# An embedding gather on GpSimd: its scratch writes and its holds give way to answers from SyncE

## The chip, the cores and the metric

One Trainium2 chip, of which the kernel uses 1 core. The metric is device time in microseconds (us), lower is better. The 16 DMA engines of the core serve all its queues. The work is done by TensorE (PE in the rows; PEld are its weight loads), VectorE (DVE), ScalarE (ACT) and GpSimd (POOL); SyncE (SP) only issues transfers.

## The reference

A recommendation model (DLRM style) for 512 samples, all in float32:

```python
B, NF, D, V, NDENSE = (512, 26, 64, 12500, 13)
h = relu(dense @ dw1 + db1)
dense_emb = relu(h @ dw2 + db2)                       # [512, 64]
sparse_emb = emb_tables[f_ids, sparse_idx]            # 26 rows of 64 floats for each sample
emb = concatenate([dense_emb[:, None, :], sparse_emb], axis=1)    # [512, 27, 64]
inter = einsum('bfd,bgd->bfg', emb, emb)
pairs = inter[:, iu0, iu1]                            # the 351 pairs above the diagonal
z = concatenate([emb.reshape(512, -1), pairs], axis=1)
z = relu(z @ ow1 + ob1)                               # 2079 -> 512
z = relu(z @ ow2 + ob2)                               # -> 256
z = relu(z @ ow3 + ob3)                               # -> 128
y = z @ ow4 + ob4                                     # -> 1
```

An index may be negative or too large; the kernel wraps and clamps it as the reference's indexing does.

## The kernel before

The 512 samples are four tiles (`t` = 0 to 3) of 128, one sample per partition. Every engine has one hand-written program, and semaphores alone set the order between them.

**GpSimd** issues 104 gathers (L211), 26 per tile, one per field. Each is an indirect DMA that brings one row of 64 floats for each of the 128 samples. The fields of a tile form four groups: `s` = 0 to 7, 8 to 15, 16 to 23, and 24 and 25. Each group has a semaphore of its own, which counts landed gathers. Behind nearly every gather stands a memset of 128x192 bytes of `pace` (L219), a scratch tensor that nothing reads; the last eight gathers of the last tile have none. In tiles 1 to 3, two gathers, `s` = 7 and `s` = 10, carry a second semaphore, `gathers_held`, and instead of a memset they are followed by a wait (L217): GpSimd stands still until TensorE has finished the first or the second half of the previous tile's interactions (`inter_done`).

**TensorE** does the following for tile `t`, in this order. `turn(t, g)` waits for group `g` and transposes its rows into a PSUM bank (L240). ScalarE (groups 0 and 2, L386 and L387) or VectorE (groups 1 and 3, L465 and L466) copies the bank into `emb`, twice. `field_products(t, g)` waits for these copies (`kept`) and multiplies them with the weights into `acc[t]` (L259), two fields at a time. `interactions(t, 0)` and `interactions(t, 1)` are 128 small products each as the trace counts them (L276), one half of the tile's samples each. ScalarE and VectorE then copy each half into `pairs` (`moves`, L392 and L182), and `pair_product(t)` (L292) adds them to `acc[t]`. The tiles overlap by a fixed list:

```python
for t in range(TILES):
    if t:
        interactions(t - 1, 0)
    turn(t, 0)
    if t:
        interactions(t - 1, 1)
    field_products(t, 0)
    if t:
        pair_product(t - 1)
        z1_to_features(t - 1, at_once)
    turn(t, 1)
    ...field_products(t, 1), turn(t, 2), field_products(t, 2), turn(t, 3), field_products(t, 3)
```

Both halves wait on `gathers_held` (L272): `interactions(t, 0)` may start only when GpSimd has issued gather `s` = 7 of the next tile and holds behind it, `interactions(t, 1)` only when it has issued `s` = 10. So no gather instruction runs beside an interaction block. The last tile's interactions come when all gathers are over and have no such wait. Layers 2 to 4 run for tiles 0 to 2 together inside the last tile, and for tile 3 at the end.

**ScalarE** works in this order around a tile's start: `moves(t - 1, 0)`, `keep(t, 0)` (the copies of group 0), `moves(t - 1, 1)`. **VectorE** first makes the row numbers of the gathers. **SyncE** issues the indices' and the first layer's weights' transfers (L190 to L194), then waits for the result (L195).

Of the kernel before, what the change touches and what calls it, by code (L numbers as in the profile page):

```python
# [7 lines left out]
NF = 26  # L8
# [6 lines left out]
P = 128  # L15
TILES = B // P
LAST = TILES - 1
# [20 lines left out]


EARLY = LAST * P  # L40
PACE = 192
HOLDS = [7, 10]
UNPACED_FROM = 18
Z1_STEPS = [(0, 1), (1, 2), (2, 4)]
K1 = H1 // P

# [21 lines left out]
def build(nc, idx, tables, dense_pack, small_pack, w1, out):  # L68
    with ExitStack() as ctx:
        def sb(name, shape, dt=F32):  # L70
            return ctx.enter_context(nc.sbuf_tensor(name, shape, dt))
# [4 lines left out]
        def sem(name):  # L76
            return ctx.enter_context(nc.semaphore(name))
# [5 lines left out]
        table_base = sb("table_base", [P, TILES, NF], I32)  # L83
        rows = sb("rows", [P, TILES, NF], I32)
        gathered = sb("gathered", [P, TILES, NF, D])
        pace = sb("pace", [P, TILES * NF, PACE], mybir.dt.uint8)
        dense_sb = sb("dense_sb", [D, DENSE_COLS])
        small = sb("small", [P, SMALL_COLS])
        dense_h = sb("dense_h", [D, B])
# [33 lines left out]
        dense_act = sem("dense_act")  # L123
        ones_set = sem("ones_set")
        group_in = [[sem(f"group_in{t}_{g}") for g in range(NG)] for t in range(TILES)]
        gathers_held = sem("gathers_held")
        group_turned = sem("group_turned")
        kept_act = sem("kept_act")
        kept_dve = sem("kept_dve")
# [1 line left out]
        inter_done = sem("inter_done")  # L131
# [56 lines left out]
        @block.sync  # L188
        def _(sp):
            sp.dma_start(idx_raw[:, 0:1, :], idx[:, 0:1, :]).then_inc(idx_in, 16)  # L190
            sp.dma_start(idx_raw[:, 1:TILES, :], idx[:, 1:TILES, :]).then_inc(later_idx_in, 16)
            for g in range(W_GROUPS):
                groups = slice(g * W_GROUP, (g + 1) * W_GROUP)
                sp.dma_start(w[:, groups, :], w1[:, groups, :]).then_inc(w_in[g], 16)  # L194
            sp.wait_ge(y_done, 2)  # L195
            sp.dma_start(out, y[:]).then_inc(y_out, 16)
            sp.wait_ge(y_out, 16)

        @block.gpsimd
        def _(pool):  # L200

            nc.gpsimd.iota(table_base[:], pattern=[[0, TILES], [V, NF]], base=0,
                           channel_multiplier=0).then_inc(base_made, 1)
            pool.wait_ge(rows_ready, 1)
            for t in range(TILES):
                if t == 1:
                    pool.wait_ge(rows_done, 1)
                for g, (c0, c1) in enumerate(GROUPS):
                    for s in range(2 * c0, 2 * c1):
                        held = t > 0 and s in HOLDS  # L210
                        pool.indirect_dma_start(  # L211
                            out=gathered[:, t, s, :], out_offset=None, in_=tables,
                            in_offset=bass.IndirectOffsetOnAxis(ap=rows[:, t, s:s + 1], axis=0),
                            engine_sem=gathers_held if held else None,
                        ).then_inc(group_in[t][g], 16)
                        if held:
                            pool.wait_ge(inter_done, 2 * (t - 1) + HOLDS.index(s) + 1)  # L217
                        elif t < LAST or s < UNPACED_FROM:
                            nc.gpsimd.memset(pace[:, t * NF + s, :], 0)  # L219

        @block.tensor
        def _(pe):
# [25 lines left out]
            def kept(t, g):  # L248

                pe.wait_ge(kept_dve if g % 2 else kept_act, t * 2 + g // 2 + 1)  # L250
                if t == LAST and g == NG - 1:
                    pe.wait_ge(kept_act, t * 2 + 3)
# [9 lines left out]
            def interactions(t, k):  # L262

                if k == 0:
                    if t == 0:
                        pe.wait_ge(dense_placed, 1)
                    kept(t, 2)
                    kept(t, 3)
                    if t:
                        moved(t - 1)  # L270
                if t < LAST:
                    pe.wait_ge(gathers_held, 2 * t + k + 1)  # L272
                for n in range(HALF):
                    for j in range(4):
                        b = t * P + j * GROUP + k * HALF + n
                        mm = nc.tensor.matmul(inter[k][QUAD * j:QUAD * j + PLACES, n * PLACES:(n + 1) * PLACES],  # L276
                                              emb[0:D, b, :], emb[0:D, b, :], start=True, stop=True)
                mm.then_inc(inter_done, 1)

            def moved(t):  # L280

                pe.wait_ge(moved_act, t + 1)
                pe.wait_ge(moved_dve, t + 1)
# [48 lines left out]
# [11 lines that stand above are left out]
                if t < LAST:  # L343
                    field_products(t, 1)
                    turn(t, 2)
                    field_products(t, 2)
                    turn(t, 3)
                    field_products(t, 3)
# [9 lines left out]
            turn(LAST, 3)  # L358
            c0, c1 = GROUPS[2]
            interactions(LAST, 0)  # L360
            field_products(LAST, 2, (c0, c0 + 2))
            interactions(LAST, 1)
# [209 lines left out]
```

## Time and profile before

| | |
|---|---|
| median of 3 runs | 188.66 us (187.79 to 189.02) |
| the profiled execution, its own time | 187.21 us |
| its span, first to last instruction | 185.4 us |
| PE busy | 127.4 us (69%) |
| POOL busy | 123.8 us (67%) |
| mean granted TensorE clock | 0.88 of full speed |
| gathers | 104, 951 ns mean, 98.9 us in all |
| scratch memsets | 90, 274 ns mean, 24.7 us in all |

A busy time says how long an engine worked, not whether anyone waited for it. The profile's chain of waits follows the work that ended last back through what released each step, and gives each its start and length. A timeline gives an engine's instructions in order of time; the brackets name how long the engine was idle before one and what released it. "Issue" is time for which the profile shows no releaser.

### The profile page before, as it was taken

What the parts mean: (1) busy time and instruction counts of PE and PEld (TensorE: products, weight loads), DVE (VectorE), ACT (ScalarE), POOL (GpSimd) and SP (SyncE); (2) the same over time, 40 slices, a digit from 0 to 9 for tenths busy, and PEclk for the clock granted to TensorE, in tenths of its full rate; (3) what the DMA queues carried; (4) which work ended last, traced back from release to release, by engine and by line L of the source; (5) the groups of instructions that cost most, each with busy time, mean ns of one, the idle gap of its engine ahead of it and who ended that gap; (6) DMA issues with size and microseconds to landing.
All of it is one profiled execution on the core that took longest, in us unless ns stands there. A gap on an engine that the chain in (4) does not pass through costs nothing.

```text
span 185.4 us, 3069 instructions
## 1 busy us (share of the span) xinstructions
PE 127.4 (69%) x1301; PEld 68.8 (37%) x1301; DVE 37.8 (20%) x97; ACT 42.2 (23%) x96; POOL 123.8 (67%) x199
## 2 busy tenths in 40 slices
PE   1510285828655995839439993959729979989994
PEld 0000132514344442524226432424426446656453
DVE  2700003000142204100144005000234023136011
ACT  0440310031046201040075001040174011166011
POOL 3888888888735888888565888888367887200000
PEclk9999999975965699996965798587997999999999
DMA  5999532221212332312312332222222324100000
GB/s 157 409 332 357 172 26 23 23 28 21 21 13 23 21 22 24 28 22 26 24 13 24 23 27 20 23 28 20 19 20 20 22 25 31 18 4 0 4 0 0
DMA packets 4576, 9.80 MB, mean 53 GB/s; under 512 B 2065, under 2 KB 2065, under 8 KB 3922
## 3 DMA queue, kind: packets, MB, share of 16 engines
q0 software_dynamic: 3328, 3.41, 21.3%
q1 hardware_dynamic: 1010, 5.30, 7.1%
q10 hardware_dynamic: 224, 0.89, 1.6%
q8 instruction: 10, 0.16, 0.4%
q14 instruction: 4, 0.03, 0.1%
HBM read 9.59 MB, written 0.00 MB: 52 GB/s over the span
## 4 chain that ended last, share of the span: by engine, by line
PE 45%; POOL 26%; issue 18%; ACT 5%; DMA 3%; DVE 2%
PE acc L259 20%; POOL gathered L211 20%; PE acc L292 10%; PE inter L276 7%; POOL pace L219 6%; PE acc L310 4%; DMA gathered<-tables,rows 2%; ACT emb L386 1%; ACT emb L387 1%; PE turned L240 1%; PE acc L301 1%; ACT pairs L392 1%; DMA idx_raw<-idx 1%; ACT z L399 1%; DVE emb L466 1%
## 5 line engine op out<-in xcount | busy, mean ns | idle before, releaser
L211 POOL DMA_INDIRECT gathered<-tables,rows x104 | 98.9, 951 | 34.6 <-issue 16.9
L259 PE MATMUL acc<-w,emb 128*128 128x512 f32 x104 | 65.7, 780 | 19.4 <-issue 12.3
L259 PEld LDWEIGHTS acc<-w,emb 128*128 128x128 f32 x104 | 31.3, 315 | 46.3 <-issue 36.9
L392 ACT ACTIVATE pairs<-inter 28x96 f32<-28x96 f32 (+1 forms) x64 | 15.7, 246 | 39.8 <-PE inter L276 39.1
L219 POOL MEMSET pace<- 128x192 uint8 x90 | 24.7, 274 | 0.1
L292 PE MATMUL acc<-w,pairs 128*128 128x512 f32 x56 | 24.7, 592 | 0.0
L182 DVE COPY pairs<-inter 28x96 f32<-28x96 f32 (+1 forms) x64 | 17.0, 266 | 26.5 <-PE inter L276 25.8
L276 PE MATMUL inter<-emb 64*28 64x28 f32 x1024 | 12.6, 204 | 13.8 <-DMA gathered<-tables,rows 10.1
L240 PE MATMUL turned<-small,gathered 128*128 128x128 f32 x52 | 10.1, 317 | 13.5 <-DMA gathered<-tables,rows 13.5
L386 ACT ACTIVATE emb<-turned 128x512 f32<-128x512 f32 x8 | 8.8, 1098 | 45.7 <-issue 28.6
L465 DVE COPY emb<-turned 128x512 f32<-128x512 f32 (+1 forms) x7 | 5.5, 784 | 64.1 <-issue 49.5
L276 PEld LDWEIGHTS inter<-emb 64*28 64x28 f32 x1024 | 11.3, 116 | 18.1 <-DMA gathered<-tables,rows 10.6
L292 PEld LDWEIGHTS acc<-w,pairs 128*128 128x128 f32 x56 | 10.6, 190 | 12.9 <-issue 12.2
L240 PEld LDWEIGHTS turned<-small,gathered 128*128 128x128 f32 x52 | 6.9, 158 | 18.6 <-issue 13.2
L399 ACT ACTIVATE z<-acc 128x512 f32<-128x512 f32 (+2 forms) x6 | 2.5, 456 | 34.8 <-PE acc L292 25.4
L387 ACT ACTIVATE emb<-turned 64x512 f32<-64x512 f32 x8 | 8.8, 1096 | 0.1
L478 DVE COPY z1t<-acc 128x512 f32<-128x512 f32 x3 | 2.1, 692 | 31.5 <-issue 20.4
L310 PE MATMUL acc<-z1t,small 128*128 128x384 f32 (+1 forms) x32 | 7.5, 387 | 0.3 <-issue 0.3
L310 PEld LDWEIGHTS acc<-z1t,small 128*128 128x128 f32 x32 | 4.8, 191 | 2.5 <-issue 0.6
L466 DVE COPY emb<-turned 64x512 f32<-64x512 f32 (+1 forms) x7 | 5.5, 790 | 0.1
L224 PE MATMUL inter<-dense_sb 13*64 13x512 f32 x2 | 2.0, 1084 | 4.0 <-DMA dense_sb<-dense_pack 4.0
L227 PE MATMUL inter<-dense_h,dense_sb 64*64 64x512 f32 x2 | 2.0, 1084 | 2.1 <-ACT dense_h L376 2.1
(47 smaller groups left out, 26.3 us busy)
## 6 DMA issues: line engine op xcount, KB each, us to landing
w<-w SPq DMA_DIRECT2D x5, 1024.0 KB, 8.7
gathered<-tables,rows POOLq DMA_INDIRECT x104, 3.4
small<-small_pack ACTq DMA_DIRECT2D x1, 706.5 KB, 6.0
dense_sb<-dense_pack ACTq DMA_DIRECT2D x1, 160.5 KB
idx_raw<-idx SPq DMA_DIRECT2D x1, 39.0 KB
idx_raw<-idx SPq DMA_DIRECT2D x1, 13.0 KB, 1.9
out<-y SPq DMA_DIRECT2D x1, 2.0 KB
```

Source lines behind the costliest of these rows:

```text
L182: last = copy(pairs[QUAD * q:QUAD * q + PLACES, t, 0:top, first:first + HALF], src)
L211: pool.indirect_dma_start(out=gathered[:, t, s, :], out_offset=None, in_=tables, in_offset=bass.IndirectOffsetOnAxis(ap=rows[:, t, s:s + 1 ...
L219: nc.gpsimd.memset(pace[:, t * NF + s, :], 0)
L240: mm = nc.tensor.transpose(turned[g % 2][:, (c - c0) * P:(c - c0 + 1) * P], gathered[:, t, 2 * c:2 * c + 2, :].rearrange("p f d -> p (f d) ...
L259: nc.tensor.matmul(acc[t][:], emb[:, tile_of(t), place(2 * c)], w[:, c, :], start=(c == 0), stop=False)
L276: mm = nc.tensor.matmul(inter[k][QUAD * j:QUAD * j + PLACES, n * PLACES:(n + 1) * PLACES], emb[0:D, b, :], emb[0:D, b, :], start=True, sto ...
L292: mm = nc.tensor.matmul(acc[t][:], pairs[:, t, s, :], w[:, FIELD_CHUNKS + s, :], start=False, stop=(s == SLOTS - 1))
L310: mm = nc.tensor.matmul(banks[m][:, 0:n], ow2[:, k, m * P:(m + 1) * P], z1t[:, k, samples], start=(k == 0), stop=(k == K1 - 1))
L386: nc.scalar.activation(evens(t, g), turned_all(g), ACT.Copy)
L387: nc.scalar.activation(odds(t, g), turned_odds(g), ACT.Copy).then_inc(kept_act, 1)
L392: last = move(lambda dst, src: nc.scalar.activation(dst, src, ACT.Copy), t, k, (0, 1))
L466: nc.vector.tensor_copy(odds(t, g), turned_odds(g)).then_inc(kept_dve, 1)
```

## The change

The memsets, the scratch tensor and both kinds of hold go: GpSimd no longer waits for `inter_done`, TensorE no longer for `gathers_held`. Instead every gather adds 1 to `gathers_issued`, SyncE waits for each such step and adds 1 to `echo` three times, and gather `n` (counted over all tiles) waits until the answers to gathers 0 to `n - 2` are complete. SyncE does this behind its weight transfers and ahead of its wait for the result.

```diff
-PACE = 192
-HOLDS = [7, 10]
-UNPACED_FROM = 18
+ECHOES = 3
+LAG = 2
...
-        pace = sb("pace", [P, TILES * NF, PACE], mybir.dt.uint8)
...
-        gathers_held = sem("gathers_held")
+        gathers_issued = sem("gathers_issued")
+        echo = sem("echo")
...
                 sp.dma_start(w[:, groups, :], w1[:, groups, :]).then_inc(w_in[g], 16)
+            for n in range(TILES * NF - LAG):
+                sp.wait_ge(gathers_issued, n + 1)
+                for _ in range(ECHOES):
+                    sp.sem_inc(echo, 1)
             sp.wait_ge(y_done, 2)
...
                     for s in range(2 * c0, 2 * c1):
-                        held = t > 0 and s in HOLDS
+                        n = t * NF + s
+                        if n >= LAG:
+                            pool.wait_ge(echo, ECHOES * (n - LAG + 1))
                         pool.indirect_dma_start(
                             out=gathered[:, t, s, :], out_offset=None, in_=tables,
                             in_offset=bass.IndirectOffsetOnAxis(ap=rows[:, t, s:s + 1], axis=0),
-                            engine_sem=gathers_held if held else None,
+                            engine_sem=gathers_issued,
                         ).then_inc(group_in[t][g], 16)
-                        if held:
-                            pool.wait_ge(inter_done, 2 * (t - 1) + HOLDS.index(s) + 1)
-                        elif t < LAST or s < UNPACED_FROM:
-                            nc.gpsimd.memset(pace[:, t * NF + s, :], 0)
...
-                if t < LAST:
-                    pe.wait_ge(gathers_held, 2 * t + k + 1)
                 for n in range(HALF):
```

## Rows read from the trace of the kernel before

**Rows 1.** Timeline of GpSimd: start us, us, engine, line, operation, idle before.
```profile
146.26 0.28 POOL L219 MEMSET pace<- 128x192 uint8 x1
146.70 0.95 POOL L211 DMA_INDIRECT gathered<-tables,rows  x1 [0.16 <-issue]
...
153.22 0.94 POOL L211 DMA_INDIRECT gathered<-tables,rows  x1 [0.30 <-issue]
```

**Rows 2.** Line L211 by itself: durations, first and last start, landings.
```profile
L211 POOL DMA_INDIRECT gathered<-tables,rows x104: 940/950/1091, 3.6 to 158.2; - x104
...
DMA to landing us min/median/max: 3.2/3.4/3.7
```

**Rows 3.** Timeline of TensorE's products.
```profile
20.52 1.08 PE L240 MATMUL turned<-small,gathered 128*128 128x128 f32 x4 [10.45 <-DMA gathered<-tables,rows]
...
32.98 3.79 PE L259 MATMUL acc<-w,emb 128*128 128x512 f32 x8 [2.43 <-issue]
39.00 0.99 PE L240 MATMUL turned<-small,gathered 128*128 128x128 f32 x4 [2.23 <-DMA gathered<-tables,rows]
42.37 5.48 PE L259 MATMUL acc<-w,emb 128*128 128x512 f32 x8 [2.38 <-issue]
...
50.62 0.48 PE L276 MATMUL inter<-emb 64*28 64x28 f32 x36 [0.47 <-DMA gathered<-tables,rows]
...
57.62 1.71 PE L276 MATMUL inter<-emb 64*28 64x28 f32 x128 [3.00 <-DMA gathered<-tables,rows]
59.26 5.58 PE L259 MATMUL acc<-w,emb 128*128 128x512 f32 x8
...
79.69 0.66 PE L240 MATMUL turned<-small,gathered 128*128 128x128 f32 x4 [0.81 <-DMA gathered<-tables,rows]
...
132.16 1.61 PE L276 MATMUL inter<-emb 64*28 64x28 f32 x128
...
139.41 4.76 PE L259 MATMUL acc<-w,emb 128*128 128x512 f32 x8
...
163.78 0.27 PE L240 MATMUL turned<-small,gathered 128*128 128x128 f32 x1
```

**Rows 4.** The chain of waits around tile 0's first interaction block: start us, us, what.
```profile
49.53 0.96 DMA gathered<-tables,rows
...
51.10 0.59 issue
...
52.39 1.19 PE inter L276 x50
```

**Rows 5.** The chain of waits around tile 1's first interaction block.
```profile
90.38 0.88 issue
...
91.78 0.82 issue
92.60 0.98 PE inter L276 x46
...
99.35 5.98 PE acc L259 x8
```

**Rows 6.** Timeline of ScalarE: the moves, then the second copy of a group 0.
```profile
53.61 2.05 ACT L392 ACTIVATE pairs<-inter 28x96 f32<-28x96 f32 x8 [11.38 <-PE inter L276]
...
56.77 1.10 ACT L387 ACTIVATE emb<-turned 64x512 f32<-64x512 f32 x1
```

**Rows 7.** Busy by stretch: length, PE, PEld, DVE, ACT, POOL, PEclk, DMA share, GB/s.
```profile
53.60:57.60 4.00, 1.02 (x4) 0.62 (x4) 2.12 (x8) 3.89 (x10) 3.39 (x5) 0.50 0.17 15
...
133.80:137.80 4.00, 0.56 (x4) 0.32 (x4) 2.13 (x8) 3.87 (x10) 3.39 (x5) 1.00 0.20 21
```

**Rows 8.** Timeline: SyncE's queue, and the copy ahead of its last transfer.
```profile
1.67 2.61 SPq L194 DMA_DIRECT2D w<-w  x5
...
183.48 0.34 DVE L489 TENSOR_SCALAR y<-inter,small 1x128 f32<-1x128 f32 x1 [1.42 <-PE inter L326]
183.85 0.32 SPq L196 DMA_DIRECT2D out<-y  x1
```

## The prediction

> **What bounds the kernel now.** I read the chain of waits first. Up to 49.5 us it runs through GpSimd alone, gather behind memset behind gather; from there on through TensorE, with three returns to GpSimd, each of three gathers, at 53.8, 93.8 and 134.1 us. So neither busy share (PE 69%, POOL 67%) is the bound; they take turns, and the questions are which of TensorE's waits are for a gather, and what is late once a gather no longer is. For this I read GpSimd's timeline for the price of one gather [rows 1, 2], TensorE's for its idle times [rows 3], and the chain at the interaction blocks [rows 4, 5].
>
> One gather takes 0.95 us on GpSimd. With a memset behind it the next one starts 0.95 + 0.28 + 0.16 = 1.39 us after it; in the tail, without memset, 0.94 + 0.30 = 1.24, say 1.25 us [rows 1]. So a memset costs 0.14 us, not 0.28: half of it covers an issue time that would be there anyway. A group counts as landed 3.4 us after its last gather's start [rows 2].
>
> **Memsets removed.** The period falls from 1.39 to 1.25 us if nothing new stands between the gathers. What this is worth is read where TensorE waits for a group. Group 2 of tile 0 ends with gather 23. It makes TensorE wait 2.23 us at 39.00 [rows 3]. Gather 23 now starts 23 x 0.14 = 3.2 us earlier, so that this wait goes whole and TensorE is bound there by its own work: -2.23 us. The same holds for the 0.81 us before the turn at 79.69 [rows 3]: -0.81. The very first turn, at 20.52, waits for gather 7, which is issued 7 x 0.14 = 1.0 us earlier; but the 5 MB of weights move in that stretch too [rows 8], and TensorE started 20.5 - 13.5 = 7.0 us after the gather's start (the first starts at 3.6 and is 1.09 long [rows 2]; 3.6 + 1.09 + 0.44 + 6 x 1.39 = 13.5) where 3.4 is usual. So the traffic has its part in that wait. Between 0 and -1.0; I take -0.4. Later tiles' groups land well before TensorE gets to them.
>
> **TensorE's holds removed.** `interactions(t, 0)` waited 0.47 us for the gather that ended at 50.49 [rows 3, 4], and 0.88 us in tile 1 [rows 5]; in tile 2 nothing (the block at 132.16 follows its products at once) [rows 3]. -0.47 - 0.88 = -1.35.
>
> `interactions(t, 1)` waited 3.00 us at 57.62 [rows 3], and about as long in the other two tiles. These are not worth 9 us. What stands behind the block is `field_products(t + 1, 0)`, and it needs ScalarE's two copies of group 0, which stand behind the moves of the first half (2.05 us); the second ends at 56.77 + 1.10 = 57.87, 57.87 - 53.58 = 4.29 us after the first block's end [rows 4, 6]; with 0.1 us to release, 4.4. Before, the products started 5.7 us after that end in tile 0 (59.26 - 53.58), 5.8 in tile 1 (99.35 - 93.58) and 5.6 in tile 2 (139.41 - 133.77) [rows 3, 4, 5]. So the wait for ScalarE takes the place of the hold, and the gain is 1.3 + 1.4 + 1.2 = 3.9 us. The second block itself (turns 1.02, block 1.71 [rows 3, 7]) fits into the 4.4 with 1.5 us to spare. The second half's moves now end on ScalarE about 4.3 + 2.1 = 6.4 us after the first block, long before the pair products, which stand behind 3.8 to 6 us of field products: nothing.
>
> **GpSimd's holds removed.** They stop GpSimd six times, but nothing on TensorE waited for the gathers behind them except the blocks already counted. Worth nothing on its own; it is the cover that the next item needs: 104 gathers at 1.25 us end near 133 us instead of 159, where TensorE needs the last group at 163.78 [rows 2, 3].
>
> **Answers added.** SyncE gets 102 waits and 306 increments, its queue is free of the weight transfers at 4.28 us [rows 8], and gather 2, the first that waits for an answer, needs that to gather 0, which ends at 3.6 + 1.09 = 4.7 [rows 2]. Behind SyncE's loop stands only the wait for the result at 183.8 us; the last answer is long over. Behind the wait on GpSimd stand only the later gathers. The increment of a gather comes at its end on the engine, not at its landing: TensorE's block started 0.13 us after the gather's end of 50.49, while its rows needed 2.4 us more [rows 2, 4]. The answer's length e isn't in the trace. From below: SyncE's last transfer starts 0.03 us after the copy that it waits for [rows 8], so e could be 0.1. From above: an increment is at most as dear as one of its weight transfers, 2.61 / 5 = 0.52 us, so three are 1.6 us and e at most 1.7. I take 0.4, near the lower end, since an increment moves no data. Gather n starts no earlier than 0.95 + 0.1 + e + 0.27 after the start of gather n - 2 (0.26 or 0.27 is what GpSimd took from the end of TensorE's block at 53.58 to its next gather at 53.84; the whole hold at 53.60 to 57.60 shows three gathers in that rhythm [rows 4, 7]), hence a period of at least 0.66 + e / 2: 0.9 us with e = 0.4, and 1.5 with 1.7. At my value the engine's own 1.25 binds, and the answer costs nothing. What covers it is the gather n - 1; if the check of the wait came only behind it and added its 0.27 each time, the period would be 1.52.
>
> **The clock.** Field products of one group took 3.79 us at the least, and 5.48, 5.58, 5.98 and 4.76 us in others [rows 3, 5], where the granted clock was at its lower level (1.2 GHz) for part of them. The stretch of the hold, with 1.0 us of TensorE work in 4.0, was granted 0.50 [rows 7], and its products began there. After the change that stretch holds both blocks closer together, and the wait before 39.00 is gone. Nothing in the rows says which low stretches stay. Between 0 and the whole of four of them (5.5 + 5.6 + 6.0 + 4.8 - 4 x 3.8 = 6.7 us); I take -1.5, since idle times of 2.4 us ahead of three products in four stay as they are.
>
> The Trainium skill bears on this ("TensorE: Matmul & The Clock Gate", part 1 on the clock gate): throttled is the default state, and activity releases it. By that rule more of the low stretches would go than I count; it is the second rival below. The trace agrees in part: 0.50 was granted in the stretch of the hold at 53.6 us, but 1.00 in that of the hold at 133.8, with less work in it [rows 7].
>
> **The sum.** -2.23 - 0.81 - 0.4 - 1.35 - 3.9 - 1.5 = -10.2 us. The profiled execution took 187.21, so it would take 177.0. That execution lies 1.45 us under the median of 188.66; by the median the forecast is 178.5 us. A difference of 1% (1.9 us) is about what a measurement of this kernel can tell from none.
>
> **Rivals.**
>
> First, the blocks and the gathers disturb each other (slower). No gather instruction of the trace runs beside an interaction block, so this cost is shown nowhere. For it: the block at 50.62 took 2.96 us, with a stall of 0.59 in it and a second like it, and that of tile 1 one of 0.82, while the last gathers were still landing [rows 4, 5]. Against it: the block at 132.16, with a gather also landing, took 1.61 us, and field products beside running gathers kept full speed at 32.98 [rows 3]. Its place is the first blocks (all of a loss x is on the path) and the second ones (x less 1.5 us of spare). With stalls of 1.1 us as in tile 0, two of three blocks already carry theirs; new would be at most 3 us. To end slower it needs 3x + 3(x - 1.5) > 12, x > 2.75 us per block, more than a block now takes. With x = 3: 178.5 + 9 + 4.5 = 192. The Trainium skill speaks against it ("SBUF — State Buffer", on the two separate sides): engine ports and DMA ports don't contend. The stalls above are no proof otherwise. I give 15%.
>
> Second, the clock comes back in full: -6.7 instead of -1.5, and 178.5 - 5.2 = 173.3 us. 13%.
>
> Third, the wait adds its 0.27 to each gather: a period of 1.52. Gather 33 then starts at 53.7 and lands at 57.1, and group 0 of tile 1 is copied by about 60, no earlier than now; gather 59 lands at 96.7, gather 85 at 136.2; the last one starts at 160.1 and lands at 163.5, where TensorE needs it at 163.78. GpSimd then sets the pace throughout and the end stays where it is: 188.5. 12%. If answers are slower still (e over 1.8, or counted from the landing, a period of (3.4 + 0.4 + 0.27) / 2 = 2.0), the end is 3.6 + 103 x period + 3.4 + 21.6 us: 195 with 1.6, over 230 with 2.0. Only this case reaches far; 4%.
>
> **How the numbers follow.** The forecast has the remaining 56%, with a range of its own of 175 to 184, the upper end from the disturbance at its small size (3 us) and no help from the clock (1.5). The range that should hold 8 times in 10 goes from 172, just past the full clock, to 189.5, past the unchanged case; 19% are left above. Faster by over 1% (under 186.8): forecast and clock and a little of the first rival, 0.71. Within 1%: 0.11. Slower: 0.18.
>
> **What would show it.** Right: GpSimd's timeline shows gathers 1.25 us apart without a break, the last near 132; no idle time of TensorE released by a gather behind the first turn; the first field products of tiles 1 to 3 start 4.4 us after the first block's end, behind ScalarE's copy. Wrong: a gap of over 0.3 us between gathers (third rival), a block L276 over 3 us (first rival), or a mean clock that moved by more than 0.02 from 0.88 (the clock term).

## The result, and the profile after

| | before | changed |
|---|---|---|
| median of 4 runs | 188.63 us (187.79 to 189.02) | 280.69 us (279.54 to 282.01) |
| ratio, 95% interval | | 1.489 [1.479, 1.499] |
| the profiled execution, its own time | 187.21 us | 282.01 us |
| its span | 185.4 us | 280.2 us |
| mean granted TensorE clock | 0.88 | 0.744 |

The change made the kernel slower by half, where 178.5 us was forecast, with 172 to 189.5 as the range. Later runs of the same program took 178 to 181 us on two chips and 285 us on a third; but first the profile of this one.

The loss has one place. Busy time in three stretches of the changed kernel (length, PE, PEld, DVE, ACT, POOL, PEclk, DMA share, GB/s):

```profile
0.00:49.30 49.30, 24.78 (x43) 10.34 (x43) 7.71 (x12) 8.57 (x9) 31.68 (x38) 0.93 0.53 147
49.30:150.80 101.50, 18.74 (x139) 10.78 (x138) 0.00 (x0) 0.00 (x0) 66.93 (x71) 0.52 0.29 24
150.80:280.20 129.40, 103.44 (x1120) 56.46 (x1120) 30.13 (x85) 33.65 (x87) 0.00 (x0) 0.85 0.01 1
```

For 101.5 us ScalarE and VectorE do nothing at all, and TensorE starts 139 products, where a block of 128 took 1.6 to 3 us before [rows 3, 4]. TensorE's timeline shows what it does in that time:

```profile
49.38 0.43 PE L275 MATMUL inter<-emb 64*28 64x28 f32 x33
51.33 0.18 PE L275 MATMUL inter<-emb 64*28 64x28 f32 x1 [1.51 <-issue]
52.05 0.18 PE L275 MATMUL inter<-emb 64*28 64x28 f32 x1 [0.54 <-issue]
53.47 0.22 PE L275 MATMUL inter<-emb 64*28 64x28 f32 x1 [1.24 <-issue]
...
142.34 0.37 PE L241 MATMUL turned<-small,gathered 128*128 128x128 f32 x1 [0.48 <-issue]
...
150.89 0.24 PE L275 MATMUL inter<-emb 64*28 64x28 f32 x1 [0.46 <-issue]
151.58 1.67 PE L275 MATMUL inter<-emb 64*28 64x28 f32 x121 [0.46 <-issue]
```

The first 33 products of `interactions(0, 0)` pass in 0.43 us. From then on one or two come at a time, and their starts lie 0.7 us or a multiple of it apart (51.33, 52.05, 53.47). TensorE waits for "issue", that is for nothing that the profile can name. At 151.58 the rest of the second block passes at once, and the crawl is over for good. What ended shortly before is the gathers:

```profile
L216 POOL DMA_INDIRECT gathered<-tables,rows x104: 938/943/1091, 3.6 to 149.0; - x104
```

The last one started at 149.0 and ended at 149.95, 1.6 us ahead of the release. It should have started at 132: most gathers stand 1.25 us apart, as forecast, but from 23 us on some waited for their answer, 1.65 us and the like, and SyncE's own steps took up to 717 ns, where they take 17 in the trace of `after_third` below:

```profile
44.39 0.94 POOL L216 DMA_INDIRECT gathered<-tables,rows  x1 [1.65 <-SPq L197]
45.64 0.94 POOL L216 DMA_INDIRECT gathered<-tables,rows  x1 [0.30 <-SPq L197]
```
```profile
L197 SPq EVENT_SEMAPHORE  x306: 2/13/717, 4.7 to 149.4; - x153
```

So TensorE and SyncE, which have nothing to do with each other there, are both slowed in steps of about 0.7 us while gathers run. The late answers also cost what the memsets' removal should have brought early on: gather 23 started at 35.23, and the turn that waits for it came at 38.63, only 0.4 us earlier than the 39.00 of before [rows 3]. The same steps are in the rows of before, if one knows what to look for: the two stalls in the block at 50.62 put its next products at 51.69 (51.10 + 0.59) and 52.39, 0.70 us apart [rows 4]. A last sign of it is that the profile knows little about the order of events here. For the longest waits of ScalarE and VectorE, 110.3 and 103.7 us, it gives "remote", which means that it found no releaser, and it gives no time to landing for the gathers, where it was 3.4 us before [rows 2]. The trace holds only 343 records of landings (a DMA's increments of a semaphore), where that of `after_third`, the same program on another chip, holds 1786. The trace of the kernel before, taken with this first measurement, isn't whole either: 1183, where `holds_7_8` below, the same kernel with one hold moved, has 1810.

### The profile page after: what moved, and what is told of

The parts are those of the page before. It is cut to its first block, busy times and chain, and to the rows that moved or that the text cites. A ratio compares the mean times of both kernels' runs of the same rounds, so it can differ in the third digit from the quotient of the medians.

```text
span 280.2 us, 3285 instructions
## 1 busy us (share of the span) xinstructions
PE 147.0 (52%) x1301; PEld 77.6 (28%) x1301; DVE 37.8 (14%) x97; ACT 42.2 (15%) x96; POOL 98.6 (35%) x109
## 4 chain that ended last, share of the span: by engine, by line
another core or an unknown queue 39%; PE 34%; ACT 9%; issue 6%; DMA 4%; SPq 3%; DVE 3%; POOL 1%
PE acc L260 18%; PE acc L291 9%; DMA gathered<-tables,rows 4%; SPq L197 3%; ACT emb L385 3%; ACT emb L386 3%; PE acc L309 3%; ACT pairs L391 2%; PE inter L275 2%; DVE emb L465 1%; POOL gathered L216 1%; DVE emb L464 1%; PE turned L241 1%; ACT z L398 1%
## 5 line engine op out<-in xcount | busy, mean ns | idle before, releaser
L216 POOL DMA_INDIRECT gathered<-tables,rows x104 | 98.2, 944 | 50.7 <-SPq L197 38.7
L260 PE MATMUL acc<-w,emb 128*128 128x512 f32 x104 | 70.0, 826 | 24.0 <-ACT emb L386 9.2
L275 PE MATMUL inter<-emb 64*28 64x28 f32 x1024 | 28.1, 202 | 85.9 <-issue 85.1
L275 PEld LDWEIGHTS inter<-emb 64*28 64x28 f32 x1024 | 19.7, 113 | 97.0 <-issue 96.0
L391 ACT ACTIVATE pairs<-inter 28x96 f32<-28x96 f32 (+1 forms) x64 | 15.8, 246 | 132.0 <-remote 110.3
L181 DVE COPY pairs<-inter 28x96 f32<-28x96 f32 (+1 forms) x64 | 17.0, 266 | 116.7 <-remote 103.7
L241 PE MATMUL turned<-small,gathered 128*128 128x128 f32 x52 | 10.2, 309 | 12.2 <-DMA gathered<-tables,rows 10.5
L457 DVE MEMSET pairs<- 128x3584 f32 x1 | 3.0, 3045 | 0.7 <-issue 0.7
```

What stands on the lines that cost most here:

```text
L181: last = copy(pairs[QUAD * q:QUAD * q + PLACES, t, 0:top, first:first + HALF], src)
L216: pool.indirect_dma_start(out=gathered[:, t, s, :], out_offset=None, in_=tables, in_offset=bass.IndirectOffsetOnAxis(ap=rows[:, t, s:s + 1 ...
L241: mm = nc.tensor.transpose(turned[g % 2][:, (c - c0) * P:(c - c0 + 1) * P], gathered[:, t, 2 * c:2 * c + 2, :].rearrange("p f d -> p (f d) ...
L260: nc.tensor.matmul(acc[t][:], emb[:, tile_of(t), place(2 * c)], w[:, c, :], start=(c == 0), stop=False)
L391: last = move(lambda dst, src: nc.scalar.activation(dst, src, ACT.Copy), t, k, (0, 1))
```

## The experiments

The kernels came in sets; each set ran on one chip, with runs of before beside it. Seven numbered chips came up; the first measurement's number isn't known. Times are us; where only one is given it is a single execution, where an interval stands there were at least four of the kernel. A chip on which no kernel crawled is called ordinary below, the others crawling chips.

### What of the change does it: first four kernels (chip 9, before 183.4)

`bare` takes the answers out of the changed kernel; neither memsets nor holds nor waits are left:

```diff
-            for n in range(TILES * NF - LAG):
-                sp.wait_ge(gathers_issued, n + 1)
-                for _ in range(ECHOES):
-                    sp.sem_inc(echo, 1)
...
-                        if n >= LAG:
-                            pool.wait_ge(echo, ECHOES * (n - LAG + 1))
...
-                            engine_sem=gathers_issued,
```

> The changed kernel without SyncE's answers, without the waits for them and without the second semaphore on the gathers: no memsets and no holds, gathers free. Theory A (TensorE gets its small products only a few at a time while gathers run, and the holds kept the two apart): the first interaction block still crawls until the last gather is out near 133 us, so 255 to 285 us. Theory B (SyncE's 306 increments and the waits disturb the engines): the block takes under 3 us and the time is the forecast's, 175 to 184 us.

`pace_only` is the kernel before without its holds, on both sides:

```diff
-                        held = t > 0 and s in HOLDS
+                        held = False
...
-                if t < LAST:
-                    pe.wait_ge(gathers_held, 2 * t + k + 1)
```

> The kernel before with its memsets behind every gather it had them and behind the formerly held ones, but without the holds on both sides. Theory A: 265 to 300 us, since the gathers go on to 148 us at 1.39 us each and the block crawls as long. Theory C (the gap that a memset makes between two gathers is what lets the other engines through): 180 to 190 us.

`holds_only` is the kernel before without its memsets:

```diff
-                        elif t < LAST or s < UNPACED_FROM:
-                            nc.gpsimd.memset(pace[:, t * NF + s, :], 0)
```

> The kernel before without memsets, with its holds. Theory A: the holds are enough; 183 to 189 us, a little faster for gathers 1.25 us apart. Theory C: the blocks or other short products crawl; over 200 us.

`echo_holds` is the changed kernel with the holds put back:

```diff
+                        if t > 0 and s in HOLDS:
+                            pool.wait_ge(inter_done, 2 * (t - 1) + HOLDS.index(s) + 1)
...
+                if t < LAST:
+                    pe.wait_ge(gathers_issued, (t + 1) * NF + HOLDS[k] + 1)
```

> The changed kernel with the holds back on both sides (after s = 7 and s = 10 of tiles 1 to 3), answers kept. Theory A: as holds_only within 1%, 183 to 190 us. Theory B: the answers disturb also here; over 200 us.

Measured: 181.7, 177.7, 173.0 and 176.5. No kernel crawled, and each single execution was faster than that of before. That spoke for theory B (the answers) against A (blocks beside gathers), but there was something to notice first: before itself took 183.4 here and 188.6 in the first measurement.

### Is it the kernel or the chip (chip 11, before 184.3)

`after_again` is the changed kernel, unchanged.

> The changed kernel itself, on the chip and beside the runs of before of this job. Theory B (the answers are the cause, whenever blocks run beside gathers): 278 to 283 us in every round. Theory D (the crawl depends on something outside the kernel that holds for a whole program on a chip, such as where it starts or which chip it is on, and the answers have no part in it): it comes out near bare, 178 to 184 us, in some or all rounds.

`echo_no_wait` lets SyncE answer, but no gather waits for it:

```diff
-                        if n >= LAG:
-                            pool.wait_ge(echo, ECHOES * (n - LAG + 1))
```

`sem_only` leaves these two lines out as well, and SyncE's four, but keeps `engine_sem=gathers_issued`.

> The changed kernel with SyncE's 306 increments kept, but the gathers don't wait for them. Theory B1 (the increments on SyncE disturb TensorE's instruction stream): about 280 us. Theory B2 (the wait of each gather for an answer is what locks the engines into steps): as bare, 178 to 184 us.

> The changed kernel without answers and waits, but each gather still adds 1 to the second semaphore at its end. If that increment at GpSimd's end is the disturbance: about 280 us. Theories B1 and B2: 178 to 184 us.

`short_holds` is `holds_only` with its second hold moved up:

```diff
-HOLDS = [7, 10]
+HOLDS = [7, 8]
```

> The kernel before without memsets and with the second hold after s = 8 instead of s = 10, so that TensorE waits for one gather instead of three ahead of its second block. By the reading of the trace the second block moves 2.5 us forward, but the field products behind it wait for ScalarE: 1.3 us less per tile than holds_only's three, 0.92 to 0.94 of before.

Measured: the changed kernel 178.4 (177.3 to 183.4 in 5 runs), a ratio of 0.969 [0.962, 0.977]; `echo_no_wait` 179.7, `sem_only` 180.5; `short_holds` 175.2, a ratio of 0.950 [0.941, 0.959], which misses the 0.92 to 0.94 expected. Theory B fell: the very program that took 280.7 took at most 183.4 here, in five executions. Theory D (something outside the kernel that holds for a whole program, such as the chip) was left.

### Ordinary chips again, with more answers (chip 12, before 184.7)

`after_third` is the changed kernel, `bare_again` is `bare`, and `echo16` has `ECHOES = 16`.

> The changed kernel once more, unchanged. Theory D (what made it crawl in its first measurement belongs to that chip or that loading of the program): 177 to 184 us on a chip where before takes 183 to 186, and 278 to 283 where before takes 188 to 189. Theory B (the kernel alone): 280 on every chip, which the earlier repetition has already made unlikely.

> No memsets, no holds, no answers, again, beside the changed kernel on the same chip. If that chip is one where the changed kernel takes 280 us, this tells the answers' part apart from the missing holds' part: 178 to 184 if the answers are needed for the crawl, 240 to 285 if blocks beside gathers are enough. On another chip 178 to 183.

> The changed kernel with 16 increments to each gather instead of 3, so about 20 more semaphore steps per us. Theory E (the engines' instructions and semaphore steps share something with a limited rate, and TensorE's small products crawl once the rate is exceeded): the crawl shows on any chip, over 220 us. Theory F (the number of increments doesn't matter; each costs SyncE 0.06 us, 16 cost 0.95 us, which is still hidden behind the gather in between): 177 to 186 us.

Measured: 181.4, 179.4 and 174.7. Five times the increments did no harm, so theory E (a limit on the number of semaphore steps, on any chip) fell for the ordinary chips. It came out faster by 6.7 us, under the 177 to 186 expected. Its granted clock was 0.928 against 0.886, and its field products took 62.4 us in all against 68.1, so that 5.7 of the 6.7 us stand in TensorE's clock; why it was granted more isn't settled. The clock tells the ordinary kernels apart elsewhere too. `bare` and `holds_only`, both on chip 9, were granted 0.877 and 0.920, and lie 8.7 us apart, with 10.5 between their field products:

```profile
L253 PE MATMUL acc<-w,emb 128*128 128x512 f32 x104 | 70.9, 834 | 20.6 <-ACT emb L379 10.6 <-DVE emb L458 10.0
L257 PE MATMUL acc<-w,emb 128*128 128x512 f32 x104 | 60.4, 724 | 19.4 <-DVE emb L464 10.0 <-ACT emb L385 9.3
```

The trace of `after_third` shows what the change does where nothing crawls. Line L216 and TensorE's timeline:

```profile
L216 POOL DMA_INDIRECT gathered<-tables,rows x104: 940/944/1091, 3.4 to 132.1; - x104
```
```profile
48.69 0.66 PE L241 MATMUL turned<-small,gathered 128*128 128x128 f32 x4 [2.15 <-DMA gathered<-tables,rows]
49.27 2.16 PE L275 MATMUL inter<-emb 64*28 64x28 f32 x128
51.68 6.57 PE L260 MATMUL acc<-w,emb 128*128 128x512 f32 x8 [0.26 <-ACT emb L386]
...
85.48 1.67 PE L275 MATMUL inter<-emb 64*28 64x28 f32 x115
88.37 0.39 PE L275 MATMUL inter<-emb 64*28 64x28 f32 x13 [1.21 <-issue]
88.69 1.11 PE L241 MATMUL turned<-small,gathered 128*128 128x128 f32 x4
89.73 1.71 PE L275 MATMUL inter<-emb 64*28 64x28 f32 x111
92.19 0.43 PE L275 MATMUL inter<-emb 64*28 64x28 f32 x17 [0.75 <-issue]
93.14 6.32 PE L260 MATMUL acc<-w,emb 128*128 128x512 f32 x8 [0.51 <-ACT emb L386]
```
```profile
L197 SPq EVENT_SEMAPHORE  x306: 17/17/17, 4.5 to 130.7; - x153
```

The last gather starts at 132.1, and every step of SyncE takes 17 ns. The field products at 93.14 wait for ScalarE and start 4.4 us after the first block's end at 88.76. But the blocks beside gathers aren't free here either: tile 1's took 3.3 and 2.9 us (85.48 to 88.76, 89.73 to 92.62). The longest of an ordinary chip took 3.7 us, in `bare` (49.81 to 53.52).

### A chip where it crawls (chip 5, before 188.1)

Three kernels again: `after_r4` the changed one, `bare_r4` as `bare`, `holds_only_3r` as `holds_only`.

> The changed kernel, unchanged, once more. Theory D (a condition of the chip of the first measurement, seen also in before: 188.6 us there against 183 to 185 on three other chips): if before takes 188 to 189 us in this job, the changed kernel takes about 280; if before takes 183 to 186, it takes 177 to 183.

> No memsets, no holds, no answers, beside the changed kernel. On a chip where the changed kernel crawls it tells whether the answers are needed for that (about 180 us) or not (over 240). Elsewhere 178 to 183.

> The kernel before without memsets, with its holds, timed: the candidate that beats both kernels. From its one look (173.0 against 183.4): 0.93 to 0.955 of before on an ordinary chip. On a chip where the changed kernel crawls, the holds should still keep blocks and gathers apart: under 0.97, unless the memsets' gaps are needed there; then over 1.0.

Measured: 284.8, 281.1 and 214.9, the last a ratio of 1.143 [1.137, 1.149] to before; before 188.1 (187.3 to 189.2 in 7 runs). This is the first measurement's behaviour. The answers aren't needed for it: without them the block crawls as well. From the timeline of `bare_r4`:

```profile
92.82 0.59 PE L268 MATMUL inter<-emb 64*28 64x28 f32 x30
95.48 0.20 PE L268 MATMUL inter<-emb 64*28 64x28 f32 x1 [2.07 <-issue]
...
130.50 0.20 PE L268 MATMUL inter<-emb 64*28 64x28 f32 x1 [2.60 <-issue]
133.31 0.20 PE L268 MATMUL inter<-emb 64*28 64x28 f32 x1 [2.60 <-issue]
```

From 97 to 139 us the products' starts are 2.8 us apart, four of the steps. And the crawl doesn't end with the gathers. The last gather of `bare_r4` ended at 133.1 (132.2 and its 0.94), but the products went on one by one, in the last 10 us at 2.1, 1.4 and at the end 0.7 us, until 149.41, 16.3 us later. In `after_r4` the last gather ended at 149.2 and the release came at 151.25:

```profile
L210 POOL DMA_INDIRECT gathered<-tables,rows x104: 940/944/1091, 3.5 to 132.2; - x104
```
```profile
148.01 0.24 PE L268 MATMUL inter<-emb 64*28 64x28 f32 x1 [0.50 <-issue]
...
149.41 1.13 PE L268 MATMUL inter<-emb 64*28 64x28 f32 x74 [0.46 <-issue]
```
```profile
L216 POOL DMA_INDIRECT gathered<-tables,rows x104: 938/942/1091, 3.4 to 148.3; - x104
```
```profile
151.25 1.71 PE L275 MATMUL inter<-emb 64*28 64x28 f32 x123 [1.87 <-issue]
```

Nor is it the gathers' own traffic. From 135.3 to 149.4 GpSimd does nothing and the DMA engines' share is 0.00, while TensorE starts nine products:

```profile
135.30:149.40 14.10, 1.89 (x9) 0.94 (x8) 0.00 (x0) 0.00 (x0) 0.00 (x0) 0.50 0.00 0
```

The gathers' packets weren't slower there either: they took 14.0% of the 16 DMA engines' 279.3 us in `bare_r4` and 21.4% of 179.9 us in `bare`, that is 626 and 616 us.

The two releases are 1.8 us apart, the ends of the gathers 16.1. So what sets the end of the crawl looks like something behind the gathers, that takes about the same time for all 104 of them however closely they are issued: (149.4 - 3.5) / 104 = 1.40 us each, an estimate. Issued 1.25 us apart, they would pile up 104 x 0.15 = 16 us, which is what `bare_r4` shows.

The trouble isn't TensorE's alone. In the two kernels that have neither memsets nor answers ScalarE starts its two copies long after the transposes that they need (in the changed kernel and `after_r4` they start within 1 us of them, at 39.33 and 38.98). ScalarE in `bare_r4`, whose transposes ended at 40.1, and in `holds_only_3r`, whose ended at 39.4:

```profile
64.69 1.09 ACT L378 ACTIVATE emb<-turned 128x512 f32<-128x512 f32 x1 [42.22 <-remote]
```
```profile
51.38 1.09 ACT L384 ACTIVATE emb<-turned 128x512 f32<-128x512 f32 x1 [28.13 <-remote]
```

By the estimate, the 34 gathers of `holds_only_3r` ahead of its first hold, of which the last ended at 45.8, leave 34 x 0.15 = 5.1 us, to 50.9; the copy started at 51.38. In the next tile the same sum is off by more: 23 gathers stand behind the second hold, the last ended at 97.7, which gives 97.7 + 23 x 0.15 = 101.2, but the copy started at 99.61. And that of `bare_r4` at 64.69 doesn't fall out of so plain a queue. There the late copies of ScalarE and VectorE (at 64.69 and 89.89) held TensorE's field products up for 26.9 and 17.2 us before the first block began:

```profile
67.03 6.50 PE L253 MATMUL acc<-w,emb 128*128 128x512 f32 x8 [26.90 <-issue]
90.83 2.06 PE L253 MATMUL acc<-w,emb 128*128 128x512 f32 x2 [17.20 <-issue]
```

In `holds_only_3r` TensorE pays for it with 14.34 us ahead of the field products, and with 11.39 in the next tile and 10.18 in the one behind; the interaction blocks, which the holds shield, run in 1.3 and 1.9 us:

```profile
53.72 6.11 PE L257 MATMUL acc<-w,emb 128*128 128x512 f32 x8 [14.34 <-ACT emb L385]
...
62.06 1.27 PE L274 MATMUL inter<-emb 64*28 64x28 f32 x128
...
67.11 1.93 PE L274 MATMUL inter<-emb 64*28 64x28 f32 x128 [3.20 <-DMA gathered<-tables,rows]
...
101.86 5.95 PE L257 MATMUL acc<-w,emb 128*128 128x512 f32 x8 [11.39 <-ACT emb L385]
```

### Are the holds needed beside the memsets

`pace_only_2` and `pace_only_3` are `pace_only`; `holds_7_8` is the kernel before with `HOLDS = [7, 8]`, memsets kept.

> The kernel before with its memsets and without the holds, once more. On a chip where before takes 188 us: if the 0.14 us that a memset adds is enough for the small products too, 180 to 186; if the blocks need the holds there, over 230. On a chip where before takes 183 to 186, as the first time: 177 to 180.

> The kernel before, memsets kept, with its second hold after s = 8 instead of s = 10, so TensorE waits for one gather of 1.39 us instead of three ahead of the second block. It keeps both protections, so it should gain on either kind of chip: 3 x 1.3 = 4 us less by the wait for ScalarE that comes next, a ratio of 0.97 to 0.985. If the engines were kept in step by the longer hold: over 1.05 on a chip where before takes 188.

> Memsets kept, holds gone, a third time, in search of a chip where before takes 188 us. There: 180 to 190 if the memsets' 0.14 us between gathers is enough, over 230 if the interaction blocks need the holds. On a chip where before takes 183 to 186: 177 to 181 as twice before.

Chip 2 (before 184.3): `pace_only_2` 180.0; `holds_7_8` 185.0, a ratio of 1.003 [1.001, 1.006], so no gain, and a miss: GpSimd now stands at both holds (1.70 and 3.50 us), its next gathers come later, and TensorE waits for the groups that they fill, 1.38 us at 52.98 and 2.81 at 118.75:

```profile
118.75 0.66 PE L240 MATMUL turned<-small,gathered 128*128 128x128 f32 x4 [2.81 <-DMA gathered<-tables,rows]
```

Chip 15 (before 186.8): `pace_only_3` 277.8. With memsets and without holds the blocks crawl there too, so that theory C (the gap that a memset makes lets the other engines through) fell for the blocks:

```profile
49.77 0.66 PE L274 MATMUL inter<-emb 64*28 64x28 f32 x41
50.91 0.18 PE L274 MATMUL inter<-emb 64*28 64x28 f32 x1 [0.49 <-issue]
51.61 0.21 PE L274 MATMUL inter<-emb 64*28 64x28 f32 x2 [0.52 <-issue]
...
150.54 1.37 PE L274 MATMUL inter<-emb 64*28 64x28 f32 x96 [0.50 <-issue]
```

The last gather started at 145.7 here and ended at 146.6, with the memsets' spacing, and the release came at 150.54, 3.9 us later and again at about the same time. ScalarE's first copy started at 39.93, as in the changed kernel.

The last run put the holds back beside the answers once more.

> The changed kernel with the holds back and the answers kept, no memsets, once more. On a chip where before takes 187 to 189: about 215 if only the memsets' wider spacing protects the other engines, under 190 if the answers do what the memsets did. On a chip where before takes 183 to 186: 174 to 178 as the first time.

It fell on an ordinary chip (7, before 183.6) and took 177.0. Whether answers with holds would do on a crawling chip what memsets with holds do was therefore not tried.

### Taken together

| kernel | memsets | holds | ordinary chips, ratio to before | crawling chips, ratio |
|---|---|---|---|---|
| before | yes | yes | 1 (183.4 to 184.7 us) | 1 (186.8 to 188.6 us) |
| `holds_only` | no | yes | 173.0 / 183.4 = 0.94 | 1.143 |
| `pace_only` | yes | no | 177.7 / 183.4 = 0.97; 180.0 / 184.3 = 0.98 | 277.8 / 186.8 = 1.49 |
| `echo_holds` | no (answers) | yes | 176.5 / 183.4 = 0.96; 177.0 / 183.6 = 0.96 | not tried |
| `short_holds` | no | yes, 7 and 8 | 0.950 | not tried |
| `holds_7_8` | yes | yes, 7 and 8 | 1.003 | not tried |
| `bare` | no | no | 181.7 / 183.4 = 0.99; 179.4 / 184.7 = 0.97 | 281.1 / 188.1 = 1.49 |
| changed | no (answers) | no | 0.969; 181.4 / 184.7 = 0.98 | 1.489; 284.8 / 188.1 = 1.51 |

Shown: on two numbered chips, as in the first measurement, TensorE's small products beside gathers come in steps of 0.7 us, and still do for some time after the gathers; it needs no answers and happens with memsets too; taking out the holds alone is enough for a ratio of 1.49 (`pace_only_3`); the holds shield the interaction blocks; ScalarE's first copies come in time with memsets or with answers, and late with neither. In all four kernels whose blocks crawled the release came between 149.4 and 151.6, whether the last gather ended at 133.1 or 149.9.

Not settled, first, whether it is the chip. Each chip came up in one set of runs only, so that something else that held for a whole set isn't ruled out. Within a set all agreed: on chip 5, three kernels and seven runs of before.

Second, what the engines share. The likely reading is a shared resource that works off a gather in about 1.40 us on such a chip. The memsets' 1.39 us keep the gathers just at that rate, so that little piles up behind them, and so do the answers, whose own lateness spreads the gathers of `after_r4` to (148.3 - 3.4) / 103 = 1.41 us. At 1.25 us a backlog grows, and it is in just these two kernels that the copies are late. But no kernel with another spacing was tried on such a chip, and the copies at 64.69 and 99.61 speak against the simplest form of it. Nor is it what moves the rows, as the DMA engines stood idle while the crawl went on.

Third, a rival that nobody tried: the recording of the events itself. `bare_r4` has 341 records of landings where `bare` has 1806, and records are missing in every trace of such a chip, which fits a path for such records that was short of room, but isn't shown. Every execution timed here has a granted clock on record, so all of them were recorded, before too. Whether these kernels crawl without a recording isn't known.

## Why the prediction was wrong

**The step that failed** is the price of the first rival, "the blocks and the gathers disturb each other": "With stalls of 1.1 us as in tile 0, two of three blocks already carry theirs; new would be at most 3 us." Measured: the first block and the one behind it took 104 us together (49.38 to 153.25) instead of some 5. I had the mechanism, its place and the rows that spoke for it, and priced it by the largest stall on show. But these stalls came with the last gathers, after which GpSimd held. How long a stall lasts when the gathers don't stop was not bounded by them. The upper bound of the unseen condition should have been "until the gathers are done", 133 us at the forecast's spacing, and even that is short of the 150 at which it ended. That price and the 15% on it set the range's upper end at 189.5. The prediction's sign for this rival, a block of over 3 us, showed at once. Its sign for the third rival, gaps of over 0.3 us between gathers, showed as well, but not for that rival's reason: most gathers kept 0.30 us, and the late ones waited for a SyncE that was itself slowed. What the engines contend for, and so why stalls of 0.6 us became a crawl of 100, stays open.

**Memsets removed.** The spacing of 1.25 us came as worked out, in every kernel without memsets whose answers weren't late. Its worth was mis-sized on ordinary chips: -3.4 us was the sum (2.23 + 0.81 + 0.4), and `holds_only` gained 10.4 in its single execution, 0.94 of before. Some 5 us of that may be the clock: its field products took 60.4 us, where those of the profiled before took 65.7, but those are of the first measurement, where the changed kernel crawled. On a crawling chip the same edit costs 27 us. That a memset "costs 0.14 us" and gives nothing in return was wrong there.

**TensorE's holds removed.** That ScalarE takes the hold's place was right: the field products start 4.4 us after the first block's end in tile 1 of `after_third`, as worked out. That the removed waits are worth 5.3 us (1.35 + 3.9) was near for `pace_only` (-5.7 and -4.3 in single executions). It doesn't add to the memsets' gain: `bare`, with both gone, gained 1.7 and 5.2 us. In the first set it lost 4.0 us against `pace_only`, while its field products took 70.9 us against 62.7, so the granted clock (0.877 against 0.913) accounts for more than the difference. Its longer blocks, up to 3.7 us, and one turn that now comes ahead of its gather (2.15 us at 48.69 in `after_third`) are part of the sum too, but weren't measured apart. "Later tiles' groups land well before TensorE gets to them" was wrong for that turn. And the wait before the turn of gather 23, which was to go whole, was still 0.43 us in `after_third`.

**Answers added.** Right on ordinary chips as far as it can be told: the answer came in time 100 times and the spacing stayed 1.25 us; the changed kernel against `bare` is +2.0 us on chip 12, within what single executions scatter. On a crawling chip, gathers waited for answers (1.65 us at 44.39, where 0.30 is the gap), which put the last one back from 132 to 149 us; but the crawl ended at 151.25 with them and at 149.41 without; `bare_r4` was 3.7 us faster than `after_r4`.

**The clock** (third-largest term, -1.5): in the crawl TensorE was granted 0.52 (stretch 49.3 to 150.8), and on ordinary chips the kernels were granted 0.88 to 0.93. The half clock follows from the crawl and isn't its cause, as blocks at half clock took 1.7 us before [rows 3, 7]. On ordinary chips this term was the least certain of all: between `holds_only` and `bare` the field products alone went from 60.4 to 70.9 us, more than the whole sum was worth.

**The Trainium skill's rule** that I weighed against the first rival ("SBUF — State Buffer", on the two separate sides) may well hold: data ports need not be what is shared. It does not speak about the delivery of instructions or semaphore steps, and I used it as if it lowered the risk of any disturbance.

The forecast of 178.5 us is what the changed kernel takes on an ordinary chip (178.4 and 181.4), but partly by luck: before takes 184 there, so that the change is worth 3%, and not the 5.4% of the sum.

## What to carry to other kernels

Waits and idle writes that keep two engines apart may guard against something that the profile shows only as small stalls at their edges; before taking them out, look for runs of short instructions that would then stand beside the other engine's stream, and price the loss by how long that stream lasts. Compare the time of the unchanged kernel from one set of runs to the next: 183.3 to 185.5 us against 186.8 to 189.2 went with the two kinds, on which the same edit gave 0.97 and 1.49. An edit that takes out a guard is to be run on several chips; here nothing that was tried on both kinds beat the kernel before on both. And a trace with many events missing is itself a finding: the kernel before already lacked a third of its landings.

## What the runs showed of the hardware that was not expected

- The first measurement and chips 5 and 15 showed it, chips 9, 11, 12, 2 and 7 did not: while gathers ran, TensorE's small products came one or two at a time at multiples of 0.70 us. It lasted until 1.6 to 16 us after the last gather's end, about 150 us in each kernel, in `bare_r4` for 14 us with the DMA engines idle. ScalarE's copies were late in the two kernels there that had neither memsets nor answers.
- A semaphore step of SyncE takes 17 ns on an ordinary chip; in a crawl steps of up to 717 ns (the first measurement) and 1377 ns (`after_r4`) stand among them.
- Landing records are missing from every trace of a crawling chip (343 in the changed kernel against 1786 on chip 12), the kernel before's among them, though its time was only 2% longer.
- On ordinary chips, too, a block of 128 small products takes up to 3.7 us beside running gathers, against 1.3 to 1.7 in `holds_only` with gathers held.
- 1632 increments by SyncE (16 per gather, 102 gathers) cost nothing that can be seen on an ordinary chip.
